# Third attention: the first batch's gathered outputs combined ahead of it, the other batches, the last normalisation and the router inside it

## What is computed

```python
# end of layer 0: each token adds two gated expert outputs
x = x + g0 * y0 + g1 * y1
# layer 1, attention: 16 heads of 64, per batch of 512 tokens
nx = layernorm(x)
q, k, v = nx @ Wq + bq, ctx @ Wk + bk, ctx @ Wv + bv
p = softmax(q @ k.T / 8)
x = x + (p @ v) @ Wo + bo
# layer 1, mixture: 16 experts, top 6
n = layernorm(x)
probs = softmax(n @ router_w.T + router_b)
gates = normalised(top6(probs))          # with EPS terms, so x also gets a small gate rest
x = x + sum over e of gates[e] * (n @ expert_w[e])
```

## Time and profile before

| | us |
|---|---|
| median of 3 runs | 1980.73 |
| lowest and highest | 1979.20, 1980.85 |
| the profiled execution, its own time | 1976.96 |
| its span | 1975.2 |
| last matmul of layer 0's mixture ends, from the span's start | 1018.4 |
| third attention's first scores begin | 1091.4 |
| its last matmul with values ends | 1723.5 |
| first matmul of the last experts begins | 1789.5 |
| last addition ends | 1967.2 |

### The profile page before, as it was taken

How to read it: one execution, slowest core, us unless ns; L and a number is a source line. 1 busy time by engine, 2 the same in 40 slices (tenths; PEclk the granted TensorE clock), 3 DMA queues, 4 the chain that set the end, 5 groups by cost and what they waited for, 6 DMA issues and landing times.

```text
span 1975.2 us, 31659 instructions
## 1 busy us (share of the span) xinstructions
PE 1720.3 (87%) x10796; PEld 1043.3 (53%) x10797; DVE 1118.6 (57%) x2989; ACT 825.1 (42%) x2001; POOL 211.6 (11%) x288
## 2 busy tenths in 40 slices
PE   4999999487887869999952999999999999977998
PEld 2555555243333659999951344444354444456886
DVE  3677777646665452222216666666656665647775
ACT  2888886425555214433321444444444443420000
POOL 0111111201111211111126000000000000020000
PEclk9999999689999869999985999999999999968999
DMA  7688885000000741111133000000000000020001
GB/s 274 235 281 284 286 298 169 21 0 1 2 1 1 269 151 35 37 36 35 37 141 102 0 1 1 1 0 1 1 1 0 1 1 1 18 68 1 0 0 43
DMA packets 55097, 140.09 MB, mean 71 GB/s; under 512 B 5856, under 2 KB 32352, under 8 KB 50240
## 3 DMA queue, kind: packets, MB, share of 16 engines
q1 hardware_dynamic: 51568, 129.20, 19.0%
q0 software_dynamic: 3408, 9.31, 1.6%
HBM read 87.25 MB, written 51.25 MB: 70 GB/s over the span
## 4 chain that ended last, share of the span: by engine, by line
PE 79%; DVE 7%; ACT 7%; issue 3%; POOL 2%; DMA 1%; SPq 0%; DVEq 0%; ACTq 0%; POOLq 0%
PE PS L658 14%; PE PS L1169 9%; PE PS L1027 7%; PE PS L1012 7%; PE PS L1096 6%; PE PS L1106 6%; PE PS L1121 6%; PE PS L856 5%; PE PS L733 4%; PE PS L755 3%; PE PS L1084 3%; PE PS L874 2%; PE PS L766 2%; POOL YP L637 2%; ACT PTf L1315 2%
## 5 line engine op out<-in xcount | busy, mean ns | idle before, releaser
L1404 ACT ACTIVATE P<-PS,nm 128x512 f32<-128x512 f32 x256 | 173.8, 683 | 318.4 <-DVE nm L1851 318.4
L1851 DVE TENSOR_REDUCE nm<-PS 128x2 f32<-128x1024 f32 x128 | 156.8, 1225 | 106.3 <-PE PS L1096 106.3
L1106 PEld LDWEIGHTS PS<-idf,P 128*128 128x128 f32 x1024 | 109.7, 141 | 104.6 <-issue 104.6
L1607 DVE CUSTOM_DVE_ANT_0 dump<-PS,maskw 128x256 f32<-128x256 f32 (+3 forms) x256 | 114.9, 488 | 82.7 <-PE PS L861 77.2
L1538 DVE CUSTOM_DVE_ANT_0 SN<-PS,SR 128x128 f32<-128x128 f32 (+3 forms) x256 | 115.4, 488 | 77.0 <-PE PS L737 76.7
L1027 PEld LDWEIGHTS PS<-xT,W1c 128*128 128x128 f32 x1248 | 148.2, 195 | 4.3 <-ACT xT L1362 2.4
L1027 PE MATMUL PS<-xT,W1c 128*128 128x128 f32 x1248 | 148.7, 278 | 1.8 <-ACT xT L1362 1.8
L856 PE MATMUL PS<-QP,KP 32*128 32x128 f32 (+3 forms) x512 | 108.8, 498 | 45.1 <-ACT PTf L1315 38.4
L1096 PE MATMUL PS<-K,Q 64*128 64x512 f32 x512 | 144.5, 641 | 0.9 <-DVE Q L1839 0.9
L1106 PE MATMUL PS<-idf,P 128*128 128x128 f32 x1024 | 139.2, 279 | 6.6 <-ACT PTb L1413 6.6
L1012 PE MATMUL PS<-EW,hT 128*128 x624 | 141.3, 379 | 1.7 <-DVE ysb L1776 1.7
(11 more groups left out here) (240 smaller groups left out, 3018.0 us busy)
## 6 DMA issues: line engine op xcount, KB each, us to landing
SR<-rel SPq DMA_DIRECT2D x16, 1024.0 KB, 8.3
rel<-EN SPq DMA_DIRECT2D x15, 1024.0 KB, 4.8
SR<-rel SPq DMA_DIRECT2D x16, 768.0 KB, 5.8
rel<-EN SPq DMA_DIRECT2D x15, 768.0 KB, 4.0
SR<-rel SPq DMA_DIRECT2D x16, 512.0 KB, 4.9
EW<-in_fc1T SPq DMA_DIRECT2D x8, 1024.0 KB, 10.8
EW<-in_fc2T SPq DMA_DIRECT2D x8, 1024.0 KB, 12.4
rel<-EN SPq DMA_DIRECT2D x15, 512.0 KB, 3.5
```

Of the source, the lines that this page charges most:

```text
L1106: last = nc.tensor.transpose(TR1[j][:, c * P:c * P + P], P1[s % 4][:, j, c * P:c * P + P], idf[:])
L1404: last = af(P1[s % 4][:, j, :], PD[s % 2][:, j, :], ACT.Exp, bias=nm1[:, s % 4, j:j + 1], accum_out=sm1[:, s % 4, j:j + 1])
L1851: v.tensor_reduce(nm1[:, s % 4, :], PD[s % 2][:], AX.X, ALU.max, negate=True).then_inc(c_max, 1)
```

## The change

Ahead of the attention only batch 0 is combined and normalised; keys of pair 0 and the four value chunks that stood in pair 0's steps are computed before that. The blocks of batches 1 to 3 are combined inside the attention, one in each step of pairs 1, 3 and 5, and normalised and transposed in pairs 2 to 7 (the bank's use "m"). The last normalisation goes by batch: statistics, one square root, normalisation and transposes (use "n") and the router's logits (use "g") lie in the steps of the next batch. The gates are computed in two parts, for 12 blocks behind step 129 and for the last 4 behind the loop. The first turn of the experts is taken apart: its 16 blocks are scattered over the steps after 128, with weights of their own in `WE0`. Loads and stores are split: keys' weights and one batch of the context first, output weights once all blocks are combined, the experts' weights in three parts, each quarter of the output as soon as it is complete. Buffers move accordingly.

```diff
-        return [r]
+        return []
...
-C_USES = [("k", 0), ("q", 0)]
+C_USES = [("k", 0)] + [("v", _i) for _i in range(RT)] + [("m", 0), ("m", 1), ("q", 0)]
...
+    C_USES += [("m", _m)] * (_r == 3 and 2 <= _m < 2 * B)
     C_USES += [("o", _b * RT + _w)] * (_r == 3 and 0 <= _b < B and _w < RT)
+    C_USES += [("n", 2 * _b + _w - 4)] * (_r == 3 and 0 <= _b < B and _w in (4, 5))
+    C_USES += [("g", _b)] * (_r == 3 and 0 <= _b < B and _w == 6)
...
+AT_OUT = [NST + RT + 7 + RT * _w for _w in range(7)]
```

On DVE, inside the loop over steps (`b, w` are `divmod(m - HP - 2, HP)` in the lines with `stats_d` and `normalise_d`):

```diff
+                if 1 <= m < 2 * B - 1 and m % 2:
+                    combine(RT * ((m + 1) // 2) + r)
+                if s in (9, 10, 17, 18, 25, 26):
+                    normalise_c0(s // 8 * 2 + s % 8 - 1)
...
+                if r == 0 and 0 <= b < B and w < RT:
+                    stats_d(b * RT + w)
+                if (r, w) in ((2, 3), (0, 4)) and 0 <= b < B:
+                    normalise_d(2 * b + w - 3)
+                if s == NST - 6:
+                    dve.wait_ge(ld["we0"], 16 * DK)
+                    dve.wait_ge(c_ot, HP * (B - 1) + 1)
+                    split_weights(0, 0)
+                if s == NST + 2:
+                    gates_d(0, 0, 12)
...
+            gates_d(1, 12, TB)
```

On ACT:

```diff
+                if s in (8, 16, 24):
+                    sqrt_c(3, s // 8)
+                if r == 3 and 2 <= m < 2 * B:
+                    tokens_c(m)
+                b, w = divmod(m - HP - 1, HP)
+                if r == 1 and 0 <= b < B and w == 4:
+                    sqrt_c(4, b)
+                if r == 3 and 0 <= b < B and w in (4, 5):
+                    tokens_d(2 * b + w - 4)
+                if m == NC1 - 1 and r < B - 1:
+                    high_part(r)
```

More of the change, by code:

```diff
@@ L70, with sums_order @@
 NTB = 4
+MIX_FIRST = [0, 1, 2, 3, 4, 5, 6, 8, 9, 10, 11, 7, 12, 13, 14, 15]
+def sums_order(order):
+    sums = [(order[0], 0)]
+    for before, tb in zip(order, order[1:]):
+        sums += [(tb, 0), (before, 1)]
+    return sums + [(order[-1], 1)]
+SUMS0 = sums_order(MIX_FIRST)
 def head_of(g, j):
@@ L1145, in _ @@
                         project_out(b * RT + w)
-            pe.wait_ge(c_gr, N_G)
-            ln_transposes(4, "ln4", lambda tb: nrm[:, tb % 4])
-            wait_all_stored(pe, "ln4")
-            bank = bank_for_write(pe, "rt1", 0)
-            for tb in range(TB):
-                for k in range(DK):
-                    last = mm(bank[:, tb * E1:tb * E1 + E1], NT[:, k, tb * P:tb * P + P], RW[:, k, :],
-                              start=(k == 0), stop=(k == DK - 1), skip_group_check=True)
@@ L1155, in _ @@
[L1155 to L1171 removed]
+                    if 0 <= b < B and w in (4, 5):
+                        tokens_c(4, "n", 2 * b + w - 4)
@@ new lines, in _ @@
+                    if 0 <= b < B and w == 6:
+                        logits_d(b)
+                if s == NST:
+                    first_turn(0)
+                if s == NST + 1:
+                    first_turn(1)
+                if s == NST + 5:
+                    first_turn(2)
+                if s == AT_OUT[0]:
+                    first_turn(3)
+                if s == AT_OUT[1]:
+                    first_turn(4)
+                if s == AT_OUT[2]:
+                    first_turn(5)
@@ new lines, in _, with turn @@
+                if s == AT_OUT[3]:
+                    first_turn(6)
+                    first_turn(8)
+                if s == AT_OUT[4]:
+                    first_turn(9)
+                if s == AT_OUT[5]:
+                    first_turn(10)
+                    first_turn(11)
+            first_turn(7)
+            for tb in range(12, TB):
+                first_turn(tb)
+            def turn(eq, i):
+                pe.wait_ge(s_ws, eq * 2 + i + 1)
+                for tb in range(TB):
+                    if tb >= 8:
+                        read = (2 * eq + i) * (2 * TB) + SUMS.index((tb - 8, 1)) + 1
+                    elif isinstance(eq, int):
+                        read = SUMS0.index((tb + 8, 1)) + 1
+                    else:
+                        read = (2 * eq + i - 1) * (2 * TB) + SUMS.index((tb + 8, 1)) + 1
+                    pe.wait_ge(s_m1, read)
+                    experts_d(i, tb)
@@ L1174, in _ @@
+            turn(0, 1)
+            with pe.Fori(1, E1 // 4) as eq:
+                for i in range(2):
+                    turn(eq, i)
         @block.scalar
@@ L1182, in ln_part @@
                     bank = bank_for_read(act, name, tb)
-                    if split:
-                        af(NThi[:, :, tb * P:tb * P + P], bank[:, 0:D].rearrange("p (k q) -> p k q", k=DK), ACT.Copy)
                     for k in range(DK):
@@ new lines, in sums_0 @@
+            def sums_0(tb, o):
+                if o == 0:
+                    dve.wait_ge(s_y1, MIX_FIRST.index(tb) + 1)
+                    dve.wait_ge(s_gc, tb + 1)
+                else:
+                    dve.wait_ge(s_m1, SUMS0.index((tb, 0)) + 1)
+                v.scalar_tensor_tensor(X[:, tb], PS[tb % 8][:, o * D:o * D + D], gat[:, tb, o:o + 1], X[:, tb],
+                                       ALU.mult, ALU.add).then_inc(s_m1, 1)
+            dve.wait_ge(ld["rows1"], 32)
+            for i in range(RT):
+                values_c(i)
@@ L1876, in _ @@
+            for tb in range(RT):
+                combine(tb)
+            for i in range(2):
+                normalise_c0(i)
             queries_c(0)
@@ L1946, in turn @@
                         split_weights(eq * 2 + i + 1, 1 - i)
+            turn(0, 1)
             dve.wait_ge(ld["we"], 16 * DK)
-            with dve.Fori(0, E1 // 4 - 1) as eq:
+            with dve.Fori(1, E1 // 4 - 1) as eq:
                 for i in range(2):
```

369 lines of the change are left out of this document (266 added, 103 removed).

## The result

| | before | after |
|---|---|---|
| median of four runs each, us | 1980.79 | 1909.26 |
| lowest and highest | 1979.20, 1987.43 | 1907.38, 1914.99 |
| ratio, 95% interval | | 0.9638 (0.9608 to 0.9668) |
| the profiled execution, its own time | 1976.96 | 1914.99 |
| its span | 1975.2 | 1913.3 |

The changed kernel is faster by 3.6%. On another chip, in six runs beside eleven of before (median 1979.1), its median was 1918.83 and the ratio 0.968 (0.9651 to 0.9709). The forecast was 1915 as a median, and 1911.5 for the profiled execution. Medians are of fast executions alone; of the experiments this leaves out one execution of after with gathers held, which took 5709.23.

A forecast was written before the change was run, and what follows sets the result against it. PE bounds the attention and last experts; two stretches with little PE work get filled. 34 + 7.4 + 44.4 + 4 - 24.4 = 65.4 us off 1976.96 gives 1911.5, as a median 1915; range 1900 to 1934.

The forecast's parts named there:

- Start, 34: From layer 0's mixture to the first scores: combining only four blocks there brings first scores at 1057.3, a gain of 34 us.
- rival (b): Ahead of the attention: the four value chunks run at half clock, 6 us later, so 1921; chance 10%.
- Combining inside, 6: Pairs 1, 3 and 5: DVE's combining costs 2.4 to 3 in pairs 1 and 5, 0.7 in pair 3; 6 us lost.
- Split 1.9: Pair 30, a plain step: splitting the first weights on DVE takes 0.68 + 1.23, so 1.9 us lost.
- POOL 3: Inside the attention: POOL's bias additions and low parts slow DVE's normalisations; 3 us lost, between 1.5 and 9.
- Rival (e): Inside the attention: POOL blocks DVE for the full length of its instructions, 6 us more, so 1921; chance 6%.
- End, 46.3: Last values to last matmul: gain 44.4 us, plus 1.9 by which two expert blocks push back the last values.
- rival (a): Six square roots inside the attention: table switches cost more than 1.28 us, 16 us in all, so 1931; chance 6%.
- (c): Inside the attention: DVE's added work isn't hidden by projections, 40 us lost instead of 24, so 1931; chance 12%.
- (d): Inside the attention: only PE's own added work counts, 12 us lost, so 1903; chance 11%.
- (f): The clock stays at 1.2 GHz into the attention, so the kernel gets slower, 1995 at 20 such steps; chance 2%.
- (g): Ahead of the attention: batch 0's gathers arrive no earlier than all do, start gains 12 us, so 1937; chance 2%.

The follow-up runs named there:

- interleaved: Changed kernel with one block's combining behind each of the four value additions ahead of the attention, not behind all four; 1917.20 us, ratio 0.9677.
- no tables: Changed kernel with six square roots inside the attention replaced by additions of the same size, so twelve table loads go; 1917.96 us, ratio 0.9690.
- lows split: Changed kernel with each of GpSimd's three subtractions of 1024 elements made as four of 256, gathers free; 1912.46 us, ratio 0.9656.
- after again: The changed kernel unaltered, run once more on chip 9; 1918.83 us, ratio 0.9680.
- all sixteen ahead: Changed kernel with all sixteen blocks combined ahead of the attention; batches 1 to 3 still normalised and transposed inside; 1934.28 us, ratio 0.9773.
- turn behind: Changed kernel with the first pair's experts and their sums moved behind the attention's end, no longer between the output projections; 1928.86 us, ratio 0.9754.
- no pairs: Changed kernel without the 24 additions of pairs of gathered outputs of batches 1 to 3 inside the attention; 1914.93 us, ratio 0.9677.
- orders only: Interleaved, plus at the end gate rests of blocks 5 to 11 behind block 12's addition and block 7's second sum before the last gates; 1909.69 us.
- warm: Interleaved, plus 28 matmuls with unused result ahead of the first keys and 8 behind the fourth value chunk; 1926.53 us, ratio 0.9713.
- all held: Orders held and lows split in one kernel; 1919.67 us, ratio 0.9706.
- after held: Changed kernel with the 24 gathers of batches 1 to 3 held until pair 0's queries have been read; 1910.40 us, ratio 0.9639.
- orders held: Orders only, with the 24 gathers of batches 1 to 3 held until pair 0's queries have been read; 1898.60 us, ratio 0.9586.

## Why the prediction was right, and where it was off

- **What bounds the kernel.** Right. The gain is what two stretches with little PE work gave back, and the attention's cost is where PE or DVE had no slack.
- **Start, 34 against 30.0.** The order was right, the clock was not: "so I take the chunks at 1.98 each" failed. Two of four ran at half clock (3.75, 3.64), and keys took 3.75: that is rival (b) for two chunks, 3.4 us of the 4.0. The continuous keys didn't raise the clock as the first projection before had. That combining starts behind the four value additions was right; interleaved shows that the data would have allowed it earlier.
- **Pair 0, 7.4 against 8.1.** Right in this trace and four others. In eight with the same instructions it was 5.2 to 6.7, where the clock was still at 1.2 GHz for the first scores or the projection behind them; in some of these late waits (last section) have a part.
- **Combining inside, 6 against 3.9.** Mechanism and places (pairs 1 and 5, 0.7 at pair 3's chunk, found at pair 4) right; too large by half. That steps with a projection hid more than I gave them is argued.
- **Uses "m" and the square roots for the queries, 4.5 against about 3.7.** Steps of pairs 1 to 8 grew by 7.6 in all, less the 3.9 of combining. Of it 1.4 is pair 4's fourth step, 6.45 for 5.01, the clash of chunk and "m" that was taken at 0.8. Square roots: nothing.
- **Last normalisation, 2.9 a batch against 2.7.** Right, with its places: pairs 13 to 16 grew by 0.93, 0.59, 1.55 and -0.33.
- **Split 1.9 against 0.9.** It stands on DVE from 1677.8 to 1679.7, the next maximum and with it ACT's copy come late, and PE waits 0.86 in step 124, which took 3.99 for 3.09; the step behind it gave 0.3 back. **POOL 3 against 1.1 to 2:** step 126 took 0.7 more than before, and the tail has the wait of 0.96; splitting gave 1.1 of both back. Rival (e) holds as a mechanism and adds nothing beyond the term.
- **End, 46.3 against 42.5.** Waits were foreseen where they are: 2.0 behind the gates (2.22), 1.9 for the norm (1.80), 3.3 at block 15 (3.69). Missing was the clock, twice: behind the first wait the projection took 5.28 for 3.62, and behind block 15's the experts' matmuls lost 1.65 more, 0.3 to 0.4 in each of four pairs and the rest in the fifth. With 0.5 that the three waits were longer, this is the whole 3.8.
- **Output, 4 against 4.6.** Right.
- **Early part, 0 against -3.8.** No term, and none could be had from the change: it is the spread of unchanged code.
- **The signs.** The combining began at 1049.8, 27.6 us behind the mixture where the prediction had 23.6 (1042.0 less 1018.4). By the letter that is past the 1048 of a wrong sign; on the time axis of before it is 1046.0. PEclk was not at 1.00 from the first queries on: these took 3.41, and at the end the clock fell twice. That the seven turns begin "about 1731" doesn't follow from the prediction's own sum: 1769.2 less the 34 + 7.4 - 24.4 gained before is 1752, and they began at 1755.6.
- **The total is partly luck.** The attention cost 6.6 less than forecast (19.7 for 24.4 + 1.9), and that covered most of the 4.0 missed at the start and the 3.8 at the end; the 3.8 of the early part nearly make up the difference of 3.5.
- **The median.** The profiled execution of before lay 3.8 under its median, that of after 5.7 over it. Worked from the same trace the forecast was 3.5 too low, as a median 5.7 too high.
- **The rule on table loads.** By "ScalarE: Activation LUTs" of the Trainium skill, each switch would have cost a drain of 1.38 more. Between busy neighbours the trace shows none:

```profile
1099.10 0.69 ACT L1513 ACTIVATE K<-PS,cols 128x512 f32<-128x512 f32 x1
1099.81 1.28 ACT L1536 ACT_TABLE_LOAD   x1
1101.10 0.30 ACT L1536 ACTIVATE sd<-mv,eps_c 128x4 f32<-128x4 f32 x1
1101.42 1.28 ACT L1521 ACT_TABLE_LOAD   x1
1102.71 0.69 ACT L1521 ACTIVATE P<-PS,nm 128x512 f32<-128x512 f32 x1
```

  With no tables, six square roots with twelve loads were worth 1.0 us in all. The measurement decides: rival (a), which had them at 16, falls.
- **Rivals (c), (d), (f), (g)** didn't occur. (c)'s 40 us of cost stand against 19.7; (d) supposed 12 and overlooked what DVE adds; (f) the granted clock was 1.00 from the first scores to the end of the 128 steps; (g) DVE didn't wait for gathers behind the fourth value addition.

## What to carry to other kernels

Work that is moved into a loop bound by one engine costs little where its step has slack on both that engine and the one that carries it, and the trace of before tells which steps these are: here the sum for 128 steps and the last values was 26.3 against a measured 19.7, with the places right. An engine's queue orders what its data don't: with one block of combining behind each value addition and the gate rests behind the addition that others wait for, first scores came 3.7 us earlier on one chip, of which 2.4 were lost again in the steps behind, and the end took 8.7 less. A short wait of PE can cost its length and 1.6 us more of half clock behind it; both falls of the clock at the end went with the waits. And compare only what ran on the same chip: the same kernel had a median of 1909.26 and 1918.83 us, and a control with the waits' supposed cause left in (lows split) was needed to see that holding the gathers proved nothing.

## What was not expected

**Late updates of semaphores.** In eight of the ten kernels whose gathers ran freely, an engine started 0.9 to 16 us later than the recorded ends of what it waited for, ahead of the first scores: 1.6 (after again), six pauses of 0.9 to 2.1 (all sixteen ahead), 1.1 (turn behind), 1.8, 3.7 and 1.8 (no tables), 4.7 (no pairs), 4.0 and 4.6 (interleaved), 2.7 and 6.0 (orders only), 16.0 (warm). In after again, turn behind and no pairs some 2 us more stood behind the first scores. All held has them in steps 4 and 5. In after, lows split, after held and orders held there are none, and from pair 3 on steps with the same instructions agree within 0.02 us in all kernels.

For most of these waits the trace has an update of the very semaphore 0.02 or 0.03 us before the start. So the engine that waited went on at once; late is the update, against the recorded end of the instruction that gives it, or this instruction itself, since ends of matmuls are modelled. In all sixteen ahead even an engine's updates to itself were late: DVE's addition ends at 1057.9, its update stands at 1059.19, its next addition starts at 1059.21.

Are the engines' own instructions late? The Trainium skill, "Runtime: NRT & Kernel Launch", section "Instruction fetch mechanics", says that each engine's sequencer fetches its program by a DMA queue of its own, in blocks of 16 KiB, mostly hidden. The profile lists queues of the kind "instruction", q8 with packets of 16384 bytes and q14 with 8192. If a late block ended a wait, a packet of such a queue should lie in it or at its end. None lies in any of the waits ahead of the first scores; in all held the two nearest stand at 1067.5 and 1067.6, 12 us ahead of its first late wait. The table of DMA queues around warm's 16 us (1052 to 1074) has the gathers alone. So these traces speak against it, as far as the two queues carry all engines' blocks, which the profile doesn't tell.

Two things go with the waits in all fourteen traces. One is the chip: all nine kernels on chips 0, 9 and 1 have them, the three on chip 4 don't, nor do before and after. It is in the medians too: 1910.40 and 1912.46 (after held, lows split) against 1914.93 to 1918.83 (no pairs, interleaved, no tables, after again). The other is the recording: the same nine traces lack most landings of the gathers, the other five have them all. The rows of queue and issue in warm (first two) and of the issue in orders held:

```profile
q0 software_dynamic: 624, 1.70, 26.9%
YP<-pair_outputs,pos POOLq DMA_INDIRECT x12
YP<-pair_outputs,pos POOLq DMA_INDIRECT x24, 2.7
```

Whether the chip delivers updates late while gathers run, or the recording of many updates both loses and delays them, is open. The runs to tell: after and after held beside each other on chip 9, and one of them timed without the profiler.

**The clock falls in short waits, and not always.** The same wait of 2.2 us ahead of the second projection at the end stands in nine traces; behind it the projection took 5.28 or 5.38 in seven and 3.69 in two (after again and no tables). Such a wait can cost 1.6 us more than itself.

**Unchanged code spreads.** Layer 0 ended between 1016.2 and 1029.9 us in thirteen traces with the same instructions up to there. Differences of a few us between kernels are worth nothing without the stretch that they come from.
